# Four score banks in a self-attention stage, two of them shared with the row maxima, and the row maxima's matmuls moved between two rounds of the mix

## What is computed

```
scores = jnp.einsum('bhtd,bhsd->bhts', q, k) / SCALE
scores = jnp.where(causal[None, None], scores, NEG_INF)
attn = jax.nn.softmax(scores, axis=-1)
mask = jnp.clip((R + z[:, :, None, None] - dist) / R, 0.0, 1.0)
attn = attn * mask
attn = attn / (attn.sum(axis=-1, keepdims=True) + 1e-08)
out = jnp.einsum('bhts,bhsd->bhtd', attn, v)
```

## Time and profile before

| | |
|---|---|
| median of the runs | 3311.54 us |
| the profiled execution | 3311.17 us, its span 3309.4 us |
| TensorE busy | 3000.5 us (91%) |
| VectorE busy | 1859.2 us (56%) |
| ScalarE, GpSimd busy | 1059.4 us, 943.3 us |
| granted clock of TensorE, mean | 0.94 |

### The profile page before, as it was taken

The page is one execution under the profiler, slowest core; times in us unless marked ns, Lnnn a source line. Parts: engine busy times, 40 slices in busy tenths (PEclk is TensorE's granted clock), DMA queues, the critical chain, the costliest instruction groups (busy, mean ns, idle before and its releaser), DMA issues. The chain is left out here.

```text
span 3309.4 us, 54872 instructions
## 1 busy us (share of the span) xinstructions
PE 3000.5 (91%) x19282; PEld 1683.9 (51%) x19282; DVE 1859.2 (56%) x2219; ACT 1059.4 (32%) x2509; POOL 943.3 (29%) x606
## 2 busy tenths in 40 slices
PE   8998899999999999999999789999999777787788
PEld 6876333333333333333333678888888333233255
DVE  4354878787887878787883345555554510000038
ACT  3222344444444444444444223333333101011023
POOL 0000544444544454444554022222221000000013
PEclk9999899999999999999999789999999897888879
DMA  4453512121212212121200411122211769999944
GB/s 166 178 203 129 127 49 67 47 68 50 64 52 55 68 49 69 46 68 52 62 14 4 156 36 64 63 68 67 71 63 57 288 258 421 420 421 420 420 154 164
DMA packets 181219, 438.54 MB, mean 133 GB/s; under 512 B 17470, under 2 KB 51928, under 8 KB 156457
## 3 DMA queue, kind: packets, MB, share of 16 engines
q1 hardware_dynamic: 174057, 425.19, 36.8%
q10 hardware_dynamic: 6976, 10.75, 0.9%
HBM read 351.74 MB, written 83.89 MB: 132 GB/s over the span
## 5 line engine op out<-in xcount | busy, mean ns | idle before, releaser
L785 ACT ACTIVATE B_e<-B_pS 128x512 f32<-128x512 f32 (+3 forms) x1280 | 617.8, 533 | 848.5 <-PE B_pS L865 423.7
L640 POOL TENSOR_TENSOR B_em<-B_e,B_mask 128x1024 f32<-128x1024 f32 (+1 forms) x320 | 671.1, 2098 | 727.7 <-ACT B_e L785 691.3
L703 DVE TENSOR_REDUCE mx<-B_pM 128x4 f32<-128x2048 f32 (+2 forms) x299 | 588.8, 1969 | 38.2 <-PE B_pM L847 19.8
L865 PE MATMUL B_pS<-B_qs,B_ks 128*128 128x512 f32 (+3 forms) x1280 | 504.8, 447 | 41.7 <-issue 18.6
L696 DVE SCALAR_TENSOR_TENSOR B_em<-B_mask,B_e 128x1024 f32<-128x1024 f32 (+1 forms) x320 | 354.8, 1109 | 255.9 <-PE B_pN L895 254.3
L865 PEld LDWEIGHTS B_pS<-B_qs,B_ks 128*128 128x128 f32 x1280 | 227.8, 192 | 362.4 <-issue 237.4
L883 PE MATMUL B_pD<-B_e,B_tiny 128*32 128x512 f32 (+3 forms) x2560 | 310.1, 557 | 0.0
L889 PE MATMUL B_pD<-B_em,B_ones 128*32 128x512 f32 (+3 forms) x2560 | 301.5, 543 | 0.7 <-DVE B_em L696 0.7
L895 PE MATMUL B_pN<-B_em,B_v 128*32 128x512 f32 (+3 forms) x2560 | 294.5, 532 | 0.0
L2089 PE MATMUL E_pI<-ring,hT 128*32 128x512 f32 x1024 | 184.7, 815 | 101.2 <-DMA ring<-in_L_ffn_e_W_dram 56.0
L2012 DVE TENSOR_TENSOR E_ug<-E_pT,bT 128x32 f32 x32 | 5.7, 192 | 445.9 <-PE E_pT L2099 445.9
(11 more groups left out here) (281 smaller groups left out, 4780.8 us busy)
## 6 DMA issues: line engine op xcount, KB each, us to landing
ring<-in_L_ffn_e_W_dram SPq DMA_DIRECT2D x128, 1024.0 KB, 21.8
ring<-in_L_ffn_e_Wg_dram SPq DMA_DIRECT2D x64, 1024.0 KB, 23.6
B_qs<-q_hi SPq DMA_DIRECT2D x64, 256.0 KB, 4.3
B_ks<-k_hi SPq DMA_DIRECT2D x64, 256.0 KB, 3.9
E_xq<-xT_sc ACTq DMA_DIRECT2D x18, 512.0 KB, 10.2
ring<-x_sc SPq DMA_DIRECT2D x36, 256.0 KB, 2.7
qc<-in_x_dram SPq DMA_DIRECT2D x34, 256.0 KB, 2.7
qc<-a_sc SPq DMA_DIRECT2D x34, 256.0 KB, 3.0
```

What stands on the lines that cost most here:

```text
L640: nc.gpsimd.tensor_tensor(em[:, f % SLOTS_EM, DVE_HEADS:, w0:], e[:, f % SLOTS_E, DVE_HEADS:, w0:], mask[:, DVE_HEADS:, u0:u0 + BLK - w0], ...
L703: nc.vector.tensor_reduce(mx[:, :, qt, c], pM[:, :, 0:w], AX.X, ALU.max).then_inc(max_taken, 1)
L785: nc.scalar.activation(e[:, f % SLOTS_E, h, w0:], pS[:, h % SBANKS, w0:], ACT.Exp, scale=SCALE).then_inc(exp_ready, 1)
L865: last = nc.tensor.matmul(pS[:, h % SBANKS, w0:], ks[:, kb // NT, h, kb % NT * P:(kb % NT + 1) * P], qs[:, qb, h, w0:], start=True, stop=( ...
```

## The change

There are four score banks. Head 0 has bank 0 of `pS` and head 3 bank 1; heads 1 and 2 use banks 2 and 3 of `pM`, which the units also write. So all 4 scores of a loop stand in a row at its head, and the unit stands inside the mix, between the rounds of `tiny` and `ones`. It waits until 3 exponentials of the loop are taken (`exps_ahead`), and the score of head 1 waits until VectorE has reduced banks 2 and 3 of the last unit (`half_taken`), for which the reduction is cut into two instructions. The turn stands behind the scores and ahead of the mix. VectorE reduces a unit before it weighs; the inverse is cut into 4 parts in 4 loops (`PARTS`) instead of 2; ScalarE copies the denominator at the end of a block's last mix loop and the numerator in the loop behind it, between heads 1 and 2.

```diff
-SBANKS = 2
+SBANKS = 4
+PARTS = 4
...
-        pS = ps("B_pS", [P, SBANKS, BLK], F32)
+        pS = ps("B_pS", [P, 2, BLK], F32)
+        score_bank = [pS[:, 0, :], pM[:, 2, :], pM[:, 3, :], pS[:, 1, :]]
...
-                nc.vector.tensor_reduce(mx[:, :, qt, c], pM[:, :, 0:w], AX.X, ALU.max).then_inc(max_taken, 1)
+                nc.vector.tensor_reduce(mx[:, 2:HPG, qt, c], pM[:, 2:HPG, 0:w], AX.X, ALU.max).then_inc(half_taken, 1)
+                nc.vector.tensor_reduce(mx[:, 0:2, qt, c], pM[:, 0:2, 0:w], AX.X, ALU.max).then_inc(max_taken, 1)
...
+                    n, later = unit_of(f)
+                    if n == 0 or (n - 1 in ENDS and not (final and later)):
+                        take_turned(rows_before(it + later, n))
+                    if not (final and later):
+                        reduce_unit(it + later, n)
                     if f == STEPS and not final:
                         dve.wait_ge(masked_last, it * STEPS + STEPS)
                         carry(dve, dve_carried)
                         ramp(it, 0, range(HPG), True)
...
-                    if f - 2 in ENDS:
-                        take(it, block_end(f - 2), 1)
+                    if f - 3 in ENDS:
+                        take(it, block_end(f - 3), 0)
...
                     if f - 2 in ENDS:
-                        take(it, block_end(f - 2), 0)
+                        take(it, block_end(f - 2), 1)
...
+            def unit(it, n, exps_ahead):
                 qb, qt, c = UNITS[n]
                 w = BLK if c < qb else (qt + 1) * P
+                pe.wait_ge(exp_ready, exps_ahead)
...
                     pe.wait_ge(exp_ready, it * HPG * STEPS + HPG * f + h + 1)
+                    if h == 1:
+                        pe.wait_ge(half_taken, units_made)
...
                 for f in range(2, STEPS + 2):
+                    n, later = unit_of(f)
                     if not final or f < STEPS:
-                        scores(it, f, (0, 1))
-                    mix(it, f - 2)
-                    n, later = unit_of(f)
+                        scores(it, f, (it + later) * STEPS + n if not (final and later) else (it + 1) * STEPS)
                     if n == 0 or (n - 1 in ENDS and not (final and later)):
                         turn(rows_before(it + later, n))
-                    if not final or f < STEPS:
-                        scores(it, f, (2, 3))
-                    if not (final and later):
-                        unit(it + later, n)
+                    exps_ahead = it * HPG * STEPS + HPG * f + 3 + SBANKS
+                    mix(it, f - 2, lambda: None if final and later else unit(it + later, n, exps_ahead))
```

More of the change, by code:

```diff
@@ L521, in self_attention @@
         max_taken = sem("B_max_taken")
+        half_taken = sem("B_half_taken")
         neg_ready = sem("B_neg_ready")
@@ L572, in _ @@
                 events.append((last - STEPS + EARLY, "high", n))
-            events += [(min(ENDS[qb] + 5, STEPS + 1), "out", qb) for qb in range(BPB)]
+            events += [(min(ENDS[qb] + 3 + PARTS, STEPS + 1), "out", qb) for qb in range(BPB)]
             events.sort()
@@ L712, in take_turned, with invert @@
                 nc.vector.tensor_copy(mrow[:, :], pM[0:ROWS, 0, 0:P]).then_inc(mrow_ready, 1)
-            def invert(it, qb, half):
+            def invert(it, qb, part):
                 dve.wait_ge(den_out, it * BPB + qb + 2)
-                at = slice(half * BLK // 2, (half + 1) * BLK // 2)
+                at = slice(part * BLK // PARTS, (part + 1) * BLK // PARTS)
                 nc.vector.reciprocal(sums[:, 1, at], sums[:, 1, at]).then_inc(inverse, 1)
@@ L720, in _ @@
             dve.sem_inc(max_taken, EARLY)
+            dve.sem_inc(half_taken, EARLY)
             dve.sem_inc(neg_ready, EARLY_ROWS)
@@ L747, in group @@
                         ramp(it, 0, range(HPG), True)
-                    n, later = unit_of(f)
-                    if n == 0 or (n - 1 in ENDS and not (final and later)):
-                        take_turned(rows_before(it + later, n))
                     if not final or f < STEPS:
                         weigh(it, f)
[L753 to L760, removed]
+                    for part in range(PARTS):
+                        if f - 3 - part in ENDS:
+                            invert(it, block_end(f - 3 - part), part)
+                    if f in plan and not final:
                         c, h = plan[f]
@@ L765, in group @@
                         ramp(it, c, [h], h == HPG - 1)
-                invert(it, BPB - 1, 0)
-                invert(it, BPB - 1, 1)
+                for part in range(PARTS):
+                    invert(it, BPB - 1, part)
             with dve.Fori(0, ITS - 1) as it:
@@ L819, in group @@
                     if f - 2 in ENDS:
-                        take(it, block_end(f - 2), 0)
+                        take(it, block_end(f - 2), 1)
+                take(it, BPB - 1, 0)
             with act.Fori(0, ITS - 1) as it:
@@ L852, in unit, with scores @@
                 last.then_inc(max_ready, 1)
-            def scores(it, f, heads):
+            def scores(it, f, units_made):
                 w0 = width(f)
                 qb, kb = FLAT[f % STEPS]
-                for h in heads:
+                for h in range(HPG):
                     if h == 0:
@@ L884, in mix @@
                                      start=first, stop=False, tile_position=(0, h * DH))
+                between()
                 pe.wait_ge(masked, it * STEPS + f + 1)
@@ L903, in _ @@
             pe.wait_ge(const_ready, 2)
-            scores(0, 0, range(HPG))
-            scores(0, 1, range(HPG))
+            scores(0, 0, EARLY)
+            scores(0, 1, EARLY)
             pe.wait_ge(mrow_ready, EARLY_ROWS)
```

17 lines of the change are left out of this document (8 added, 9 removed).

## The result

The changed kernel takes 3423.71 us (median of 4 runs, 3418.67 to 3430.35) beside 3308.75 us of the kernel before on the same chip (4 runs, 3304.58 to 3311.75): a ratio of 1.0342, with a 95% interval of 1.0327 to 1.0356. The forecast was 3306, with a range that ended at 3340. It was wrong by 118 us.

A forecast was written before the change was run, and what follows sets the result against it. TensorE, busy 91% of the span, was taken to bound the kernel, two score banks costing it 0.35 us in a full loop. Seven passes +5, last pass -15.6, clock +5: -5.6 us on 3311.17, forecast 3306, range 3280 to 3340.

The forecast's parts named there:

- 8 plain full: Full attention loops 15 to 19 and 30 to 32: 4.43 us each instead of 4.82, -3.1 us per pass.
- 3 behind a block's end: Loops 6, 14, 26: ScalarE's copies delay the third exponential to 2.75 us and the unit waits: +1.54 us per pass.
- 4 with a turn: Loops 5, 21, 25, 33: turn ahead of the mix, unit waits for the copy of the turned rows: +1.86 us per pass.
- end of a pass: Loops 40 to 3: VectorE's chain still bounds, with loop 4 starting at 23.1 us against 23.2: -0.1 us per pass.
- the sum for VectorE: Full loops: reductions 2.3, weighing 1.2, at most 0.9 for inversion or ramp: 4.4 us in a loop of 4.43.
- VectorE becomes the bound: Rival: ramps of 0.73 us, not 0.48, make `half_taken` late, 0.3 in 12 loops: +25 us, 3331; chance 0.11.
- The sum for a loop on TensorE: Plain full loop: unit at 2.2, 0.40 to `ones`, `ones` 0.86, numerator 0.97: 4.43 us, 0.39 less than 4.82.
- The wait on three exponentials: `exps_ahead` holds each loop's unit until some 2.2 us; TensorE's chain arrives at 2.11, just late enough.
- full loops of the last pass: From loop 21 on, without units: 3.83 us instead of 4.81, ten loops saving 9.9 of the last pass's 15.6 us.
- rival of late starts: Rival: `ones` 0.10 later behind waiting units, +20 us, with the clock's full bound +11 more: 3337; chance 0.20.
- `0.05 for the wake-up`: In the unit's wait for the third exponential: 0.05 us added after it ends, within the 2.17 us sum.
- 5 for the clock: End of a pass: rest of loop 3 possibly at a lower clock, 0.7 us per pass, +5 us for seven.

The follow-up runs named there:

- GpSimd reads little: Changed kernel, GpSimd multiplying only the first 16 columns of a step and filling the rest with ones (weights of heads 2 and 3 left out): 3290.62 us, ratio 0.9945.
- GpSimd second: GpSimd's weighing waits for VectorE's of the same loop: on the changed kernel 3391.4 us; on the kernel before, with the reduction ahead of the weighing, 3400.51 us.
- + ramps ahead: Changed kernel with GpSimd weighing after VectorE, and VectorE's ramps moved ahead of its weighing: 3306.61 us, ratio 0.9989.
- best: On top of + ramps ahead: turned rows copied right behind the block-ending reduction, ScalarE's numerator copy behind all four exponentials: 3271.19 us, ratio 0.9877.
- Both edits: Same run as + ramps ahead: 3306.61 us. Of its edits on the changed kernel, GpSimd's order alone took 3391.4 us, the ramps alone 3430.35.

## Why the prediction was wrong

I set the forecast per kind of loop beside five kernels, in us per pass against the kernel before. Each is the mean of seven passes, worked out from the starts of the first scores; a pass is counted from its loop 4 to loop 4 of the next, so that its end is loops 40 to 3. The kinds and the forecast are those of the prediction.

| loops | forecast | changed | GpSimd reads little | GpSimd second | + ramps ahead | best |
|---|---|---|---|---|---|---|
| 8 plain full | -3.1 | +1.34 | -2.89 | -1.39 | -2.88 | -2.87 |
| 29 | -0.27 | -0.18 | -0.25 | +0.12 | +0.12 | +0.13 |
| 5 with a diagonal unit | -0.44 | -0.17 | -0.48 | -0.12 | -0.46 | -0.46 |
| masked or narrow scores | +0.14 | +1.85 | +0.15 | +1.83 | +0.15 | +0.15 |
| 4 with a narrow mix | +1.12 | +1.31 | +1.30 | +1.31 | +1.30 | +1.30 |
| 3 behind a block's end | +1.54 | +3.64 | +1.00 | +1.21 | +1.29 | -0.30 |
| 4 with a turn | +1.86 | +7.88 | +2.46 | +9.04 | +2.90 | -0.15 |
| end of a pass | -0.1 | +0.92 | -1.99 | +0.91 | -1.80 | -1.80 |
| together | +0.75 | +16.59 | -0.70 | +12.91 | +0.62 | -4.02 |

The sums close on the whole. Seven passes of the changed kernel lose 116.2 us, the last one from its loop 4 gains 9.8, what stands ahead of the first pass's loop 4 loses 3.4 and what stands behind the last matmul gains 1.5: 108.2, the difference of the spans. In three of the seven passes of the kernel before, loop 26 takes 1.6 us more than in the others, with 3.4 us of the clock at 1.2 GHz in it; without these the loops behind a block's end read +1.7 with GpSimd's reads gone, close to the forecast.

**The step that failed** is the sum for VectorE: "2.3 (two halves for the 2.23 of the earlier trace rows) + 1.2 for its weighing + at most 0.9 for a quarter of the inversion [...] or a ramp = 4.4 in a loop of 4.43". The 2.3 held, and the quarter of the inversion too (0.94). The 1.2 is the duration of a weighing while GpSimd doesn't weigh. I took it from a trace in which the two were mostly apart, for a kernel in which one event releases both, and this is visible without a run: the change puts the exponentials of heads 2 and 3 ahead of the mix, and in the kernel before GpSimd's weighing waited for little else (691.3 of 727.7 us of its idle time, above). At full width that weighing costs 1.89 in the mean and up to 3.4, so VectorE has 5.1 in such a loop and not 4.4. The cost showed in the earlier trace rows: a ramp of 0.73 us where 0.47 is usual. I used it as the price (0.3 us) of a rival with a chance of 0.11, instead of asking what had stretched it. GpSimd's row of that moment in the kernel before answers: its weighing ends at 1054.69, and the ramp ends at 1054.97, the same 0.28 behind it as the blocked ramp above. 57 of the 128 ramps of the kernel before end so.

```profile
1052.32 2.37 POOL L640 TENSOR_TENSOR B_em<-B_e,B_mask 128x1024 f32<-128x1024 f32 x1 [2.44 <-ACT B_e L785]
```

That rival, VectorE becomes the bound, named the right engine, with `half_taken` late as it said; its size, 3331, came from the smallest case of the collision.

The Trainium skill (SBUF — State Buffer, Who interferes with whom) states this rule, and I did not bring it to the prediction: VectorE and GpSimd share one port pair to SBUF, an instruction holds it to its end, and the one issued second is blocked meanwhile; it names VectorE instructions with two SBUF inputs, against a GpSimd instruction that reads SBUF, and those in a two-port mode. The traces agree: 1.08 us behind GpSimd's end in one order and 3.41 for 2.38 in the other, and no harm to the reductions from PSUM (2.22 us).

**How slower weighings became 115 us.** The weighings take 159 us more (513.7 less 354.8), and TensorE's row of waits shows what comes late behind them: `half_taken` (63.7 us in all, in 67 places) and the copy of the turned rows (48.6, in 29). Both edits together leave 16.2 and 24.0. The clock falls behind such waits: in loop 33 TensorE stands idle for 2.15 us ahead of 1119.36, and the records have it at 1.2 GHz from 1118.6 for 6.8 us. In the whole stage they have 158.5 us at 1.2 GHz, in 35 stretches, against 83.9 us in 11 before, and 69.9 us in 14 with both edits. Work done in 74.6 more microseconds at half speed takes at most 37.3 us longer, so of the 110.1 us that the stage grew by at least 72 are not the clock's; they are waits for the most part. The share of each was bounded and not isolated, for no run held the clock.

```profile
PE B_pM L874 <- DVE mx L706: 63.7, 67, 7.2
PE B_pM L854 <- DVE B_mrow L717: 48.6, 29, 2.1
```

**What held.** The sum for a loop on TensorE, 4.43, is 4.46. With both edits one loop reads 0.33 + 0.47 + 0.33 = 1.13 for the scores (forecast 1.12), the unit at 2.16 behind the first score (2.2), 0.44 from it to `ones` (0.40, bounds 0.33 and 0.44), 0.89 and 0.97:

```profile
972.09 0.50 PE L875 MATMUL B_pS<-B_qs,B_ks 128*128 128x512 f32 x1
972.42 0.62 PE L875 MATMUL B_pM<-B_qs,B_ks 128*128 128x512 f32 x2
972.89 0.40 PE L875 MATMUL B_pS<-B_qs,B_ks 128*128 128x512 f32 x1
973.22 1.07 PE L893 MATMUL B_pD<-B_e,B_tiny 128*32 128x512 f32 x8
974.25 0.51 PE L855 MATMUL B_pM<-kh,qh 32*128 32x512 f32 x4
974.69 1.06 PE L900 MATMUL B_pD<-B_em,B_ones 128*32 128x512 f32 x8
975.58 1.04 PE L906 MATMUL B_pN<-B_em,B_v 128*32 128x512 f32 x8
976.55 0.50 PE L875 MATMUL B_pS<-B_qs,B_ks 128*128 128x512 f32 x1
```

The wait on three exponentials is real: ScalarE's second and third end at 974.20 (973.12 + 1.08), and the unit starts at 974.25.

```profile
973.12 1.08 ACT L790 ACTIVATE B_e<-B_pM 128x512 f32<-128x512 f32 x2
```

The full loops of the last pass are 3.85 (1880.62 to 1884.47) in the changed kernel itself, 3.83 forecast, since no unit waits for VectorE there:

```profile
1880.62 0.50 PE L874 MATMUL B_pS<-B_qs,B_ks 128*128 128x512 f32 x1
...
1884.47 0.50 PE L874 MATMUL B_pS<-B_qs,B_ks 128*128 128x512 f32 x1
```

With both edits the last pass takes 148.3 us from its loop 4 (1667.3 to 1815.6), 13.1 less than the 161.4 before; 15.6 was forecast. Loop 12 is 3.60 (3.55), and loop 33 is 6.42 (6.0) in the kernel in which GpSimd reads little, the one free of the collision.

The rival of late starts fell. It had `ones` come 0.10 later behind a unit that waited. With both edits this unit waited for 0.42 us, and `ones` starts 0.44 behind it, as behind the one at 974.25 above; over the stage it is 0.43 to 0.44 behind all 32 full-width units that waited over 0.1 us.

```profile
965.79 0.51 PE L855 MATMUL B_pM<-kh,qh 32*128 32x512 f32 x4 [0.42 <-ACT B_e L790]
966.23 0.43 PE L900 MATMUL B_pD<-B_em,B_ones 128*32 128x128 f32 x8
```

**Smaller misses.** The end of a pass gains 1.8 us with both edits, where -0.1 was forecast. Its sum had a term of "2.04 us to go back to the loop's start", and that was misread: the 2.04 of the earlier trace rows is a wait for TensorE's numerator round (`<-PE B_pN`), which stood ahead of VectorE's first weighing. In the new order a reduction comes first, and VectorE goes on without a gap:

```profile
1102.24 3.38 DVE L723 RECIPROCAL B_sums<-B_sums 128x128 f32<-128x128 f32 x4
1105.54 1.17 DVE L707 TENSOR_REDUCE mx<-B_pM 128x2 f32<-128x1024 f32 x1
```

This half reduction ends 17.7 us behind the start of loop 40 (1089.02), where the sum had 19.7. The loops with a turn take 1.0 us of it back (+2.90 for +1.86). The `0.05 for the wake-up` had no row behind it; the unit above starts 0.05 behind the exponential.

With both edits the span is 6.7 us below the kernel before, and the forecast was 5.6 (3306.6 us measured, 3306 forecast). That these agree is luck: the seven passes give +4.3 where 10 was forecast (5, and 5 for the clock), the last pass -13.1 for -15.6, and ahead of the first pass's loop 4 stands +1.7 that the forecast didn't have. It says nothing for the forecast of the change as it was made. Of the expectations, those for GpSimd second (in both kernels) missed for a like reason as the prediction: I costed the repair of one blocked instruction, and the next one on the same engine took its place.

## What to carry to other kernels

Before a duration is taken from a trace, see what ran on the neighbour engine meanwhile, and whether the change keeps these two apart; look in particular for two instructions that come to be released by the same event. When VectorE and GpSimd both work on data in SBUF, give them an order, with the one that others wait for first, and put the instructions that the trace shows unharmed (here the reductions from PSUM and the inversions) where they overlap. Judge such repairs together, since one alone (32 us, or nothing) hid what both were worth (117). And before a gap is taken for a fixed cost, read what ended it: the 2.04 us at the end of a pass were a wait.

## What the hardware showed

- A VectorE weighing (128x1024, two inputs in SBUF) that starts behind GpSimd's ends 1.08 us after it (151 of 151 in the changed kernel), though it takes 1.20 to 1.23 alone; in the other order by as little as 0.02 to 0.05 us, GpSimd's takes 3.41 instead of 2.37, that is 1.04 more. A few hundredths decide which engine pays.
- A ramp or its clip (one input in SBUF) is blocked in the same way: 2.33 to 2.60 us for 0.43 to 0.47, ending 0.28 us behind GpSimd's end. Reductions from PSUM are not: 2.22 us beside GpSimd and 2.23 away from it. Nor is a quarter of the inversion (one input in SBUF too): the 34 that run wholly beside GpSimd's weighing in the changed kernel take 0.94 to 0.95 us, as elsewhere.
- A row-tiled unit between two column-tiled rounds costs 0.43 to 0.44 us to the next round, as much as in front of a full-array score, although the weights of that round are 32 columns wide. By the prediction's estimate from the Trainium skill (TensorE: Matmul & The Clock Gate, LDWEIGHTS) it would be 0.36, and the trace doesn't agree. The loads themselves do agree with the page: 0.11 us for 32 columns and 0.19 for 128 in the changed kernel, 0.08 apart as its rule has it. What failed is the step from the load to the distance of the starts.
